# A two-layer graph kernel: diagonal blocks loaded once, and the norms and scaling of finished panels moved to other engines

## Chip, core and metric

The kernel runs on one core of one Trainium2 chip. The metric is the device time of one execution in microseconds: a median of 2270.47 us over 3 runs of the kernel before (2269.53 to 2271.97). TensorE is PE in the profile, VectorE DVE, ScalarE ACT, GpSimd POOL, and SyncE SP.

## What is computed

Everything is float32; N is 8192 rows, D is 128 columns, and adj is a full 8192 x 8192 matrix (256 MB).

```python
# layer 0
A = a * adj, with (1 - a) added to its diagonal
y = (A @ x) / A.sum(axis=1)
x1 = layernorm(x + relu(y @ W.T + b))
# layer 1, on x1
xt  = logmap0(x1)
par = adj   * sigmoid(xt @ wp[:D] [:, None] + xt @ wp[D:] [None, :] + b_par)
chi = adj.T * sigmoid(xt @ wc[:D] [:, None] + xt @ wc[D:] [None, :] + b_chi)
u   = chi @ xt + par @ xt
n   = max(norm(u), 1e-15)
e   = tanh(n) * u / n            # expmap0, then proj: norm at most 1 - 1e-5
out = layernorm(x1 + e * min(1, MAXNORM / norm(e)))
```

Layer 1 needs each block of adj twice: as it stands and turned. Of a block on the diagonal both are the same block of memory.

## The kernel before

adj is cut into 8 panels of 1024 output columns (`NPAN`, `BP`). A **unit** is one tile of 128 rows of layer 1 against one panel of 1024: 512 units. Two units share one load of 1 MB of the natural blocks (`a_cols`, kind "nat") and one of the turned ones (`g_blk`, kind "trn"). The loads go through a ring of 7 entries of 1 MB, to which three more in `xA` are added at the end of layer 0; `load_plan` writes the order out by hand, and SP issues each load once the last user of its entry is done (`wait_free`).

While layer 0 streams its 256 pairs, 154 units of the first three panels are interleaved. The other 358 units, from `N_EARLY` = 154, are the late stage. One unit of it is, on each engine:

- ACT: two sigmoids of 128x1024, one into `chi(n)` in SBUF (L646), one into a PSUM slot (L660). There are three slots; the sigmoid into a slot waits for the key of its last user.
- POOL: chi times the natural block (L494).
- DVE: the slot times the turned block (`first_product`, L914), then the sum of the two into `keys(n)` (`key`, L925).
- PE: two matmuls with `xtA`, accumulated in `outp` over a panel (L1125; four records each unit).

Panels 3 to 7 run 64 units each; between them the last 8 units of panels 0 to 2 are done. A group that ends releases its panel's **final**. Their base units b are 232, 266, 304, 338, 376, 410, 448 and 512 (`FINALS`), for the panels 3, 0, 4, 1, 5, 2, 6, 7. Of each final, the steps stand at fixed units after b (the constants `F_...`), written into each engine's order ahead of that unit's work:

- ACT copies `outp` to `uT` (L684; for the early panels it was done by L689), PE turns it by eight 128x128 transposes into a slot (`turn`, L1137), ACT copies the slot to `uN` in SBUF (L694) and takes eight squares with sums, one in each of eight units (L699).
- ACT takes the root of the eight sums (L707), together with the deviation of the final before (L712); each such visit needs a load of ACT's table and one back. DVE works out the factor in eight steps of 128x8 (`factor_step`, L939 to L953), with a tanh of ACT between steps 1 and 2 (L717).
- DVE turns the deviation of the final before into a factor and a shift (L973, L978), and ACT normalises that final's rows in eight pieces (L724), from b + 20 on.
- POOL scales `uN` by the factor (L510) and adds x1 (L516), at b + 29 and b + 31. DVE takes the statistics, one of eight in each of eight units (L960), and merges them (L967).

The chain of one final hangs on the next one's steps for its deviation and normalisation. The last final (b = 512) runs after the last unit, with nothing beside it.

Of the kernel before, what the change touches and what calls it, by code (L numbers as in the profile page):

```python
# [11 lines left out]
P = 128  # L12
# [48 lines left out]
def plan():  # L61

    unit_at, units, ends, waiting = {}, [], [], []
    groups = early_groups()
    for k, (p, tiles, a) in enumerate(groups):
        for jt in tiles:
            waiting.append((k, p, jt, (a + 1) * PPP + (T_OWN if p == a else T_UNITS)))
    for g in range(PAIRS):
        if waiting and waiting[0][3] <= g:
            k, p, jt, _ = waiting.pop(0)  # L70
            unit_at[g] = len(units)
            units.append((k, p, jt))
    n_early = len(units)
    units += [(k, p, jt) for k, p, jt, _ in waiting]
    order = []
    for k in range(EARLY, NPAN):
        order.append((k, range(UPP)))
        if k - EARLY < EARLY:
            order.append((k - EARLY, range((NPAN - 1) * TPP, UPP)))
    for p, tiles in order:  # L80
        groups.append((p, tiles, NPAN - 1))
        units += [(len(groups) - 1, p, jt) for jt in tiles]
    for n, (k, _, _) in enumerate(units):
        if n + 1 == len(units) or units[n + 1][0] != k:
            ends.append(n)
    return unit_at, units, n_early, groups, ends
# [5 lines left out]
LATE0 = N_EARLY  # L92

# [10 lines left out]
def finals():  # L104
# [30 lines left out]
def slot_plan():  # L135

    of_unit, of_final, holder, turn = {}, {}, {0: ("layer 0", 0), 1: ("passage", 0), 2: None}, 0
    starts = {b + F_SLOT: k for k, (_, b) in enumerate(FINALS)}
    uses = []
    for n in range(UNITS):  # L140
        if n in starts:
            uses.append(("final", starts[n], n))
        uses.append(("unit", n, n))
    uses.append(("final", len(FINALS) - 1, UNITS))
    last = 2
    for kind, i, n in uses:
        if n < SLOT_TWO:
            s = 2
        elif n < SLOT_THREE:
            s = 0 if last == 2 else 2  # L150
        else:
            s = (last + 1) % SB
        last = s
        (of_unit if kind == "unit" else of_final)[i] = (s, holder[s])
        holder[s] = (kind, i)
    return of_unit, of_final


SLOT_OF_UNIT, SLOT_OF_FINAL = slot_plan()
# [101 lines left out]
def adj_resnorm_kernel(nc, x_g, xT, g_blk, a_blk, WT, b_row, alpha, w_par, b_par, w_chi, b_chi, out):  # L261
    with ExitStack() as ctx:
# [38 lines left out]
        fs = sb("fs", [P, 11, UPP])  # L301
        mvf = sb("mvf", [P, UPP, 2])
        bstf = sb("bstf", [P, TPP, 6])
        s_n, s_nm, s_th, s_rn, s_s1, s_n2, s_s, s_sd, s_rs, s_mb, s_ss = [fs[:, k, :] for k in range(11)]
# [3 lines left out]
        uN = dsum[:, BP:2 * BP]  # L308
# [74 lines left out]
        p_ready = sem("p_ready")  # L383
        m1_ready = sem("m1_ready")
# [6 lines left out]
        uN_ready = sem("uN_ready")  # L391
# [5 lines left out]
        scaled = sem("scaled")  # L397
# [9 lines left out]
        N_CONST = 9  # L407

# [3 lines left out]
        def _(sp):  # L412
            def wait_free(e, before):
# [63 lines left out]
        def _(pool):  # L477
# [27 lines left out]
            def scale(k):  # L505
                at = slice(k * TPP, (k + 1) * TPP)
                u3 = uN.rearrange("p (t d) -> p t d", t=TPP)
                pool.wait_ge(f_step, f_steps(k, F_STEPS))
                pool.wait_ge(sq_ready, k + 1)
                pool.tensor_tensor(out=u3, in0=u3, in1=s_s[:, at].unsqueeze(2).to_broadcast([P, TPP, D]),  # L510
                                   op=ALU.mult).then_inc(scaled, 1)

            def add_residual(k):
                pool.wait_ge(scaled, k + 1)
                pool.wait_ge(x1f_in[k % 2], 16 * (k // 2 + 1))
                pool.tensor_tensor(out=x1f[k % 2][:, :], in0=uN, in1=x1f[k % 2][:, :], op=ALU.add).then_inc(v_ready, 1)  # L516

# [8 lines left out]
            for n in range(N_EARLY, UNITS):  # L526
                if n == LATE0 + 2 * T_FOLD:
                    fold(NPAN - 1)
                for k, (_, b) in enumerate(FINALS):
                    if n == b + F_SCALE:  # L530
                        scale(k)
                    if n == b + F_ADD:
                        add_residual(k)
# [3 lines left out]
            scale(NPAN - 1)  # L537
            add_residual(NPAN - 1)

        @block.scalar  # L540
        def _(act):
# [93 lines left out]
            def sigmoids(n):  # L635
# [12 lines left out]
                s, before = SLOT_OF_UNIT[n]  # L648
                if before is not None:
                    kind, i = before  # L650
                    if kind == "unit":
                        act.wait_ge(k_ready, i + 1)
                    elif kind == "final":
                        act.wait_ge(uN_ready, i + 1)
                    elif kind == "layer 0":
                        act.wait_ge(y_evac, NPAN)
                    else:
                        act.wait_ge(rows_ready, NPAN)
                        act.wait_ge(prcr_ready, NPAN)
                act.activation(slots[s], scores[:, row, 0, :], ACT.Sigmoid,  # L660
# [18 lines left out]
            def evacuate(k):  # L679
# [3 lines left out]
                act.wait_ge(sq_ready, k)  # L683
# [7 lines left out]
            def copy_turned(k):  # L691
                act.wait_ge(uT_ready, k + 1)
                act.wait_ge(v_ready, k)
                act.activation(uN, slots[SLOT_OF_FINAL[k][0]], ACT.Copy).then_inc(uN_ready, 1)  # L694

            def square(k, i):
                if i == 0:
                    act.wait_ge(uN_ready, k + 1)
                ins = act.activation(uT[:, i * D:(i + 1) * D], uN[:, i * D:(i + 1) * D], ACT.Square,  # L699
                                     accum_out=s_ss[:, k * TPP + i:k * TPP + i + 1])  # L700
                if i == TPP - 1:
                    ins.then_inc(sq_ready, 1)

            def norm(k):
                at = slice(k * TPP, (k + 1) * TPP)
                act.wait_ge(sq_ready, k + 1)
                act.activation(s_n[:, at], s_ss[:, at], ACT.Sqrt).then_inc(f_norm, 1)  # L707
# [20 lines left out]
            def final(k, step):  # L728
                if step == F_EVAC and FINALS[k][0] >= EARLY:
                    evacuate(k)  # L730
                if step == F_COPY:
                    copy_turned(k)
                if F_SQUARE <= step < F_SQUARE + TPP:
                    square(k, step - F_SQUARE)
# [53 lines left out]
            copy_turned(k)  # L788
            for i in range(TPP):
                square(k, i)  # L790
# [8 lines left out]
        def _(dve):  # L799
# [109 lines left out]
            def first_product(n):  # L909
                t, here, count = loaded("trn", n // 2)  # L910
                dve.wait_ge(here, count)
                dve.wait_ge(p_ready, n + 1)
                s = slots[SLOT_OF_UNIT[n][0]]
                dve.tensor_tensor(out=s, in0=s, in1=half(t, n), op=ALU.mult).then_inc(m1_ready, 1)  # L914

            def key(n):
                dve.wait_ge(m1_ready, n + 1)
                dve.wait_ge(m2_ready, n + 1)
                b, before = buffer_of(n, KB)
                if before is not None:  # L920
                    dve.wait_ge(kt_used, before + 1)
                elif b == KB:
                    dve.wait_ge(l0_used, PAIRS)
                    dve.wait_ge(res_ready, NPAN)
# [4 lines left out]
            def factor_step(k, i):  # L929
# [24 lines left out]
                ins.then_inc(f_step, 1)  # L954

# [25 lines left out]
            def final(k, i):  # L981
# [8 lines left out]
                if k > 0 and i == F_RSTD + 1:  # L990
                    final_shift(k - 1)
                if F_STATS <= i < F_STATS + TPP:
# [41 lines left out]
            for i in range(F_STEPS):  # L1034
                factor_step(k, i)
            for i in range(TPP):
# [6 lines left out]
        def _(pe):  # L1043
# [84 lines left out]


            def turn(k):  # L1130
                p, b = FINALS[k]
                pe.wait_ge(out_evac, GROUP_OF_FINAL[k] + 1)
                s, (kind, i) = SLOT_OF_FINAL[k]
                src = uT if p >= EARLY else acc[:, p * BP:(p + 1) * BP]
                pe.wait_ge(k_ready, i + 1)
# [55 lines left out]
```

## Time and profile before

| what | value |
|---|---|
| median of 3 runs | 2270.47 us (2269.53 to 2271.97) |
| profiled execution | 2267.84 us |
| its span, first to last instruction | 2266.0 us |
| busy: PE, DVE, ACT, POOL | 87%, 88%, 60%, 60% |
| bytes moved | 839.19 MB, 370 GB/s over the span |
| granted TensorE clock, mean | 0.972 |

An engine's row of the timeline gives an instruction's start and duration; two that follow each other without a wait overlap by some 0.1 us, so the cost of one is the distance between two starts. A releaser ("<-ACT ps L660") is whose semaphore ended the wait; "issue" means that the view found none.

### The profile page before, as it was taken

Reading aid. Unit: us, or ns where it says so; the run is one execution under the profiler, and the core shown is the slowest. Engines: PE = TensorE matmul, PEld = TensorE weight load, DVE = VectorE, ACT = ScalarE, POOL = GpSimd, SP = SyncE. Lnnn points to the kernel's source line nnn. Section 1 sums busy time; section 2 is a strip of 40 time slices with the busy share of each in tenths; the row PEclk is TensorE's granted clock in tenths of the full one; section 3 lists DMA queues with packets and bytes.
Section 4 is the critical chain, followed back from the end, with each engine's and each line's share of the span. In section 5 each row is a group of like instructions: output and inputs, shape, how many; then the busy total and the mean of one; then the engine's idle time right before and its main releaser. Section 6 shows DMA issues by size and latency. Waiting matters only on the chain. (4 is left out here: it accounts for less than half of the span.)

```text
span 2266.0 us, 17584 instructions
## 1 busy us (share of the span) xinstructions
PE 1964.4 (87%) x4652; PEld 829.8 (37%) x4652; DVE 1983.8 (88%) x1881; ACT 1349.4 (60%) x1640; POOL 1355.3 (60%) x559
## 2 busy tenths in 40 slices
PE   8999999999999989989999867887777778777774
PEld 3444444444444434434434323232222223222221
DVE  4676978988989988998999888999999999999995
ACT  0011324344364454453453687998889899898986
POOL 0000305436455455543444777999898998989995
PEclk9999999999999999999999988999999999999998
DMA  9998989899899988988888998999999999999993
GB/s 309 340 351 308 371 296 385 359 355 396 325 372 417 382 338 353 375 348 343 371 347 351 420 410 317 399 420 421 421 389 421 420 406 414 399 423 396 421 398 127
DMA packets 132083, 839.19 MB, mean 370 GB/s; under 512 B 15232, under 2 KB 27776, under 8 KB 33680
## 3 DMA queue, kind: packets, MB, share of 16 engines
q1 hardware_dynamic: 125184, 817.94, 90.5%
q10 hardware_dynamic: 6800, 20.13, 2.3%
q8 instruction: 38, 0.62, 0.1%
q14 instruction: 61, 0.50, 0.1%
HBM read 829.56 MB, written 8.45 MB: 370 GB/s over the span
## 5 line engine op out<-in xcount | busy, mean ns | idle before, releaser
L494 POOL TENSOR_TENSOR chi<-chi,ring 128x1024 f32<-128x1024 f32 x320 | 819.0, 2569 | 662.5 <-ACT chi L646 598.8
L1125 PE MATMUL ps<-keys,xtA 128*128 128x512 f32 x1720 | 847.1, 620 | 189.0 <-DVE keys L925 170.5
L1056 PE MATMUL ps<-ring,xA 128*128 128x512 f32 x2048 | 921.5, 600 | 37.1 <-DMA ring<-in_g_blk 32.9
L660 ACT ACTIVATE ps<-scores,prcr 128x1024 f32<-128x1024 f32 x512 | 567.8, 1109 | 435.9 <-DVE keys L925 417.4
L823 DVE TENSOR_TENSOR dsum<-dsum,ring 128x2048 f32<-128x2048 f32 x240 | 592.8, 2470 | 43.5 <-DMA ring<-in_g_blk 36.3
L914 DVE TENSOR_TENSOR ps<-ps,ring 128x1024 f32<-128x1024 f32 x440 | 537.7, 1222 | 66.6 <-ACT ps L660 62.7
L925 DVE TENSOR_TENSOR keys<-ps,chi 128x1024 f32<-128x1024 f32 x430 | 526.5, 1224 | 72.2 <-issue 39.4
L1056 PEld LDWEIGHTS ps<-ring,xA 128*128 128x128 f32 x2048 | 387.0, 192 | 531.3 <-issue 469.5
L1125 PEld LDWEIGHTS ps<-keys,xtA 128*128 128x128 f32 x1720 | 316.6, 195 | 688.2 <-issue 664.1
L646 ACT ACTIVATE chi<-scores,prcr 128x1024 f32<-128x1024 f32 x430 | 488.4, 1136 | 14.5 <-DMA scores<-plcl_d 6.7
L494 POOL TENSOR_TENSOR chi<-chi,xA 128x1024 f32<-128x1024 f32 x110 | 259.0, 2367 | 41.5 <-ACT chi L646 39.6
L1125 PE MATMUL ps<-xA,xtA 128*128 128x512 f32 x328 | 171.2, 647 | 49.1 <-DVE xA L925 33.6
L494 POOL TENSOR_TENSOR xA<-xA,ring 128x1024 f32<-128x1024 f32 x50 | 118.4, 2368 | 6.8 <-ACT xA L646 6.4
L1125 PEld LDWEIGHTS ps<-xA,xtA 128*128 128x128 f32 x328 | 60.4, 202 | 154.6 <-issue 135.0
L925 DVE TENSOR_TENSOR xA<-ps,xA 128x1024 f32<-128x1024 f32 x82 | 100.4, 1224 | 3.5 <-POOL xA L494 0.8
L487 POOL TENSOR_TENSOR dsum<-dsum 128x1024 f32<-128x1024 f32 x8 | 18.8, 2354 | 137.8 <-DVE dsum L823 137.8
L914 DVE TENSOR_TENSOR ps<-ps,xA 128x1024 f32<-128x1024 f32 x72 | 87.9, 1221 | 12.2 <-ACT ps L660 12.2
L646 ACT ACTIVATE xA<-scores,prcr 128x1024 f32<-128x1024 f32 x82 | 93.1, 1135 | 0.4 <-ACT yb L599 0.4
L558 ACT ACTIVATE small<-mv,epsc 128x8 f32<-128x8 f32 x8 | 2.4, 301 | 149.1 <-DVE mv L857 149.1
L494 POOL TENSOR_TENSOR xA<-xA 128x1024 f32<-128x1024 f32 x32 | 75.8, 2368 | 5.1 <-ACT xA L646 4.4
L819 DVE TENSOR_TENSOR dsum<-ring 128x1024 f32<-128x1024 f32 x16 | 34.4, 2186 | 31.4 <-PE ps L1065 17.2
L503 POOL TENSOR_TENSOR acc<-taken,acc 128x1024 f32<-128x1024 f32 x15 | 37.4, 2491 | 31.0 <-ACT taken L676 31.0
(99 smaller groups left out, 645.7 us busy)
## 6 DMA issues: line engine op xcount, KB each, us to landing
ring<-in_g_blk SPq DMA_DIRECT2D x476, 1024.0 KB, 9.8
ring<-in_a_cols SPq DMA_DIRECT2D x185, 1024.0 KB, 9.0
xA<-in_a_cols SPq DMA_DIRECT2D x71, 1024.0 KB, 9.5
xA<-in_g_blk SPq DMA_DIRECT2D x36, 1024.0 KB, 10.8
scores<-plcl_d ACTq DMA_DIRECT2D x22, 512.0 KB, 11.2
xA<-in_x_g SPq DMA_DIRECT2D x64, 64.0 KB, 13.2
yb<-in_xT ACTq DMA_DIRECT2D x8, 512.0 KB, 8.9
x_d<-res ACTq DMA_DIRECT2D x8, 512.0 KB, 9.0
```

Source lines behind the costliest of these rows:

```text
L487: pool.tensor_tensor(out=dsum[:, 0:BP], in0=dsum[:, 0:BP], in1=dsum[:, BP:2 * BP], op=ALU.add).then_inc(folded, 1)
L494: pool.tensor_tensor(out=chi(n), in0=chi(n), in1=half(t, n), op=ALU.mult).then_inc(m2_ready, 1)
L503: pool.tensor_tensor(out=at, in0=taken[:, :], in1=at, op=ALU.add).then_inc(acc_added, 1)
L558: act.activation(std, mv[:, :, 1], ACT.Sqrt, bias=epsc[:, 0:1]).then_inc(std_ready, 1)
L646: act.activation(chi(n), scores[:, row, 1, :], ACT.Sigmoid, bias=prcr[:, 2 * jt + 1:2 * jt + 2]).then_inc(c_ready, 1)
L660: act.activation(slots[s], scores[:, row, 0, :], ACT.Sigmoid, bias=prcr[:, 2 * jt:2 * jt + 1]).then_inc(p_ready, 1)
L819: dve.tensor_tensor(out=half(dsum, h), in0=half(t0, h), in1=half(t, h), op=ALU.add) \
L823: dve.tensor_tensor(out=dsum[:, :], in0=dsum[:, :], in1=t, op=ALU.add).then_inc(deg_added, 1)
L914: dve.tensor_tensor(out=s, in0=s, in1=half(t, n), op=ALU.mult).then_inc(m1_ready, 1)
L925: dve.tensor_tensor(out=keys(n), in0=slots[SLOT_OF_UNIT[n][0]], in1=chi(n), op=ALU.add).then_inc(k_ready, 1)
L1056: ins = pe.matmul(Y[:, h * BANK:(h + 1) * BANK], xA[:, tile * D:(tile + 1) * D], t[:, tt * BP + h * BANK:tt * BP + (h + 1) * BANK], start= ...
L1125: ins = pe.matmul(outp[:, h * BANK:(h + 1) * BANK], xtA[:, jt * D:(jt + 1) * D], keys(n)[:, h * BANK:(h + 1) * BANK], start=begins, stop=i ...
```

## The change

For the five late panels (3 to 7), the 8 units whose tile lies in the panel's own block ("own", 40 units in all, the list `OWN`) go last in their group. For those, the turned load is not made: 20 loads of 1 MB fewer. PE turns the natural block into the unit's PSUM slot instead (`turn_own`, eight transposes each unit, two units ahead), and ACT's sigmoid goes to one of two SBUF buffers (`own_par`: `taken` and the piece of `xA` that was the fourth buffer of `keys`). `keys` has three buffers throughout.

Of a finished panel, ACT squares the unturned `uT` (or `acc`) in one instruction into `sqT`, PE sums the squares over the partitions by eight matmuls with a column of ones into a slot (`norms`), and ACT takes the root from there. PE turns the panel into another slot later, and DVE multiplies by the factor and adds x1 in eight instructions that read PSUM (`add_residual`). ACT's copy and eight squares, and POOL's two instructions, are gone. The steps stand at new places.

```diff
+        if len(tiles) == UPP:
+            own = range(p * TPP, (p + 1) * TPP)
+            tiles = [jt for jt in tiles if jt not in own] + list(own)
-F_EVAC, F_TURN, F_SLOT, F_COPY, F_SQUARE, F_ROOT, F_FLOOR, F_INV, F_RSTD, F_TANH, F_CHAIN, F_NORM, F_SCALE, F_ADD, \
-    F_STATS, F_AGGR = 3, 2, 4, 5, 6, 15, 17, 18, 18, 19, 21, 20, 29, 31, 33, 42
+F_EVAC, F_SQUARE, F_NORMS, F_NORMS_SLOT, F_ROOT, F_FLOOR, F_INV, F_RSTD, F_TANH, F_CHAIN, F_NORM, F_TURN, F_SLOT, \
+    F_ADD, F_STATS, F_AGGR = 3, 4, 4, 6, 7, 8, 9, 9, 12, 11, 13, 14, 16, 17, 18, 26
-F_STORE = 42
-L_ROOT, L_RSTD, L_NORM = 47, 49, 52
+F_STORE = 36
+L_ROOT, L_RSTD, L_NORM = 34, 36, 38
-        kinds += [("nat", c), ("trn", c)]
+        kinds += [("nat", c)] if 2 * c in OWN_AT else [("nat", c), ("trn", c)]
-            b, _ = buffer_of(n, KB)
-            return keys_few[:, b, :] if b < KB else xA[:, EXTRA * CH + BP:EXTRA * CH + 2 * BP]
+            return keys_few[:, n % KB, :]
+        own_par = [taken[:, :], xA[:, EXTRA * CH + BP:EXTRA * CH + 2 * BP]]
...
+                    if 2 * j in OWN_AT:
+                        sp.wait_ge(own_turned, (OWN_AT[2 * j] // TPP + 1) * TPP)
...
-            scale(NPAN - 1)
-            add_residual(NPAN - 1)
...
+                if n in OWN_AT:
+                    i = OWN_AT[n]
+                    if i >= 2:
+                        act.wait_ge(m1_ready, OWN[i - 2] + 1)
...
+            def square(k):
+                p, _ = FINALS[k]
+                act.wait_ge(out_evac, GROUP_OF_FINAL[k] + 1)
+                act.wait_ge(norms_ready, k)
+                act.activation(sqT, uT if p >= EARLY else acc[:, p * BP:(p + 1) * BP], ACT.Square).then_inc(sq_ready, 1)
...
+                if n in OWN_AT:
+                    dve.wait_ge(own_turned, OWN_AT[n] + 1)
+                    other = own_par[OWN_AT[n] % 2]
...
+            def add_residual(k):
+                dve.wait_ge(f_step, f_steps(k, F_STEPS))
+                dve.wait_ge(uT_ready, k + 1)
+                dve.wait_ge(x1f_in[k % 2], 16 * (k // 2 + 1))
+                for i in range(TPP):
+                    t, j = x1f[k % 2][:, i * D:(i + 1) * D], k * TPP + i
+                    ins = dve.scalar_tensor_tensor(out=t, in0=slots[SLOT_OF_FINAL[k][0]][:, i * D:(i + 1) * D],
+                                                   scalar=s_s[:, j:j + 1], in1=t, op0=ALU.mult, op1=ALU.add)
+                ins.then_inc(v_ready, 1)
...
+            def turn_own(n):
+                s, before = SLOT_OF_UNIT[n]
+                slot_free(pe, before)
+                for k in range(TPP):
+                    (t, here, count), h = natural_of_own(n, k)
+                    pe.wait_ge(here, count)
+                    ins = pe.transpose(columns(slots[s], k), columns(half(t, h), UNIT[n][2] % TPP), ident[:, :])
+                ins.then_inc(own_turned, 1)
+
+            def norms(k):
+                pe.wait_ge(sq_ready, k + 1)
+                s, before = SLOT_OF_NORMS[k]
+                slot_free(pe, before)
+                for j in range(TPP):
+                    ins = pe.matmul(slots[s][:, j:j + 1], columns(sqT, j), ones[:, 0:1], start=True, stop=True)
+                ins.then_inc(norms_ready, 1)
...
+                    if n == b + F_NORMS:
+                        norms(k)
...
+                if n + 2 in OWN_AT:
+                    turn_own(n + 2)
```

## Rows read from the trace of the kernel before

**Rows 1.** The page: busy time of each engine, then GB/s in 40 slices.

```profile
PE 1964.4 (87%) x4652; PEld 829.8 (37%) x4652; DVE 1983.8 (88%) x1881; ACT 1349.4 (60%) x1640; POOL 1355.3 (60%) x559
...
GB/s 309 340 351 308 371 296 385 359 355 396 325 372 417 382 338 353 375 348 343 371 347 351 420 410 317 399 420 421 421 389 421 420 406 414 399 423 396 421 398 127
```

**Rows 2.** L914 in two windows: us, busy (count), clock, DMA share, GB/s.

```profile
1422.90:1494.90 72.00, 36.67 (x30) 0.99 1.00 413
1494.90:2237.10 742.20, 340.53 (x279) 0.97 0.99 405
```

**Rows 3.** DVE's waits, 1494.9 to 2237.1: us in total, times, longest.

```profile
DVE keys L925 <- issue: 13.1, 6, 2.2
DVE ps L914 <- ACT ps L660: 11.9, 17, 2.1
DVE keys L925 <- DVE ps L914: 4.1, 7, 0.6
DVE keys L925 <- POOL chi L494: 3.5, 14, 0.3
```

**Rows 4.** DVE's groups there: count, busy us, mean ns, idle before.

```profile
L943 DVE TENSOR_TENSOR fs<-fs 128x8 f32<-128x8 f32 x7 | 9.5, 1358 | 0.0
...
L939 DVE TENSOR_SCALAR fs<-fs 128x8 f32<-128x8 f32 x7 | 7.3, 1041 | 0.0
...
L945 DVE TENSOR_TENSOR fs<-fs 128x8 f32<-128x8 f32 x7 | 3.2, 462 | 0.0
...
L960 DVE BATCH_NORM_STATS2 bstf<-yb 128x6 f32<-128x128 f32 x32 | 9.1, 284 | 0.0
...
L967 DVE BATCH_NORM_AGGREGATE mvf<-bstf 128x2 f32<-128x6 f32 x56 | 4.4, 151 | 0.0
```

**Rows 5.** Timeline, first final: start, us, engine, operation, idle before.

```profile
1550.02 4.65 POOL L494 TENSOR_TENSOR chi<-chi,ring 128x1024 f32<-128x1024 f32 x2
...
1554.63 2.35 POOL L494 TENSOR_TENSOR xA<-xA,ring 128x1024 f32<-128x1024 f32 x1
...
1554.71 2.30 DVE L945 TENSOR_TENSOR fs<-fs 128x8 f32<-128x8 f32 x1
```

**Rows 6.** Timeline of the third final, ACT's square root and normalisation.

```profile
1723.95 1.28 ACT L707 ACT_TABLE_LOAD   x1
...
1729.21 1.23 DVE L914 TENSOR_TENSOR ps<-ps,ring 128x1024 f32<-128x1024 f32 x1 [2.09 <-ACT ps L660]
...
1740.33 0.49 ACT L724 ACTIVATE res<-res,fs 128x128 f32<-128x128 f32 x1 [2.77 <-DVE fs L978]
```

**Rows 7.** Timeline of DVE, the eight products that read PSUM in layer 0.

```profile
1304.19 2.15 DVE L845 SCALAR_TENSOR_TENSOR res<-ps,small,bb 128x128 f32<-128x128 f32 x8
```

**Rows 8.** Timeline of PE around a turn, and the degree sums' matmuls.

```profile
1501.74 1.88 PE L1125 MATMUL ps<-keys,xtA 128*128 128x512 f32 x4
1503.46 1.11 PE L1137 MATMUL ps<-ident,dsum 128*128 128x128 f32 x8
1504.41 1.88 PE L1125 MATMUL ps<-keys,xtA 128*128 128x512 f32 x4
...
1274.94 1.70 PE L1065 MATMUL ps<-ones,dsum 128*128 128x1 f32 x14
```

**Rows 9.** Timeline of the last final, after the last unit.

```profile
2241.74 1.02 ACT L684 ACTIVATE dsum<-ps 128x1024 f32<-128x1024 f32 x1 [7.57 <-PE ps L1125]
...
2248.89 0.21 ACT L707 ACTIVATE fs<-fs 128x8 f32<-128x8 f32 x1
...
2252.01 1.90 POOL L510 TENSOR_TENSOR dsum<-dsum,fs 128x1024 f32<-128x1024 f32 x1 [15.37 <-DVE fs L953]
...
2256.36 1.65 DVE L960 BATCH_NORM_STATS2 bstf<-res 128x6 f32<-128x128 f32 x8 [4.42 <-POOL res L516]
```

**Rows 10.** What the SP queue waited for from 1494.9 to 2237.1.

```profile
SPq L470 <- POOL chi L494: 493.2, 133, 6.4
```

**Rows 11.** Issues of that window: KB each, us from issue to landing.

```profile
ring<-in_a_cols SPq DMA_DIRECT2D x81, 1024.0 KB, 9.7
```

More of the change, by code:

```diff
@@ L92 @@
 LATE0 = N_EARLY
+OWN = [n for n in range(N_EARLY, UNITS) if UNIT[n][1] >= EARLY and UNIT[n][2] // TPP == UNIT[n][1]]
+OWN_AT = {n: i for i, n in enumerate(OWN)}
 def is_first(n):
@@ L135, in slot_plan @@
 def slot_plan():
-    of_unit, of_final, holder, turn = {}, {}, {0: ("layer 0", 0), 1: ("passage", 0), 2: None}, 0
-    starts = {b + F_SLOT: k for k, (_, b) in enumerate(FINALS)}
+    plans = {"unit": {}, "norms": {}, "final": {}}
+    holder = {0: ("layer 0", 0), 1: ("passage", 0), 2: None}
+    starts = {b + F_NORMS_SLOT: ("norms", k) for k, (_, b) in enumerate(FINALS)}
+    starts |= {b + F_SLOT: ("final", k) for k, (_, b) in enumerate(FINALS)}
     uses = []
@@ L141, in slot_plan @@
         if n in starts:
-            uses.append(("final", starts[n], n))
+            uses.append(starts[n] + (n,))
         uses.append(("unit", n, n))
-    uses.append(("final", len(FINALS) - 1, UNITS))
+    uses += [("norms", len(FINALS) - 1, UNITS), ("final", len(FINALS) - 1, UNITS)]
     last = 2
@@ L153, in slot_plan @@
         last = s
-        (of_unit if kind == "unit" else of_final)[i] = (s, holder[s])
+        plans[kind][i] = (s, holder[s])
         holder[s] = (kind, i)
-    return of_unit, of_final
-SLOT_OF_UNIT, SLOT_OF_FINAL = slot_plan()
+    return plans["unit"], plans["norms"], plans["final"]
+SLOT_OF_UNIT, SLOT_OF_NORMS, SLOT_OF_FINAL = slot_plan()
 def load_plan():
@@ L300, in adj_resnorm_kernel @@
          dg, sf, rc, inv, mb) = [small[:, k, :] for k in range(21)]
-        fs = sb("fs", [P, 11, UPP])
+        fs = sb("fs", [P, 10, UPP])
         mvf = sb("mvf", [P, UPP, 2])
         bstf = sb("bstf", [P, TPP, 6])
-        s_n, s_nm, s_th, s_rn, s_s1, s_n2, s_s, s_sd, s_rs, s_mb, s_ss = [fs[:, k, :] for k in range(11)]
+        s_n, s_nm, s_th, s_rn, s_s1, s_n2, s_s, s_sd, s_rs, s_mb = [fs[:, k, :] for k in range(10)]
         uT = dsum[:, 0:BP]
-        uN = dsum[:, BP:2 * BP]
+        sqT = dsum[:, BP:2 * BP]
         x1f = [yb, res]
@@ L407, in adj_resnorm_kernel, with slot_free @@
         N_CONST = 9
+        def slot_free(eng, before):
+            kind, i = before
+            if kind == "unit":
+                eng.wait_ge(k_ready, i + 1)
+            elif kind == "norms":
+                eng.wait_ge(f_norm, i + 1)
+            elif kind == "final":
+                eng.wait_ge(v_ready, i + 1)
+            elif kind == "layer 0":
+                eng.wait_ge(y_evac, NPAN)
+            else:
+                eng.wait_ge(rows_ready, NPAN)
+                eng.wait_ge(prcr_ready, NPAN)
         block = ctx.enter_context(nc.Block())
@@ L647, in sigmoids @@
                                bias=prcr[:, 2 * jt + 1:2 * jt + 2]).then_inc(c_ready, 1)
[L648 to L656, printed above, removed]
-                    else:
-                        act.wait_ge(rows_ready, NPAN)
-                        act.wait_ge(prcr_ready, NPAN)
-                act.activation(slots[s], scores[:, row, 0, :], ACT.Sigmoid,
+                if n in OWN_AT:
+                    i = OWN_AT[n]
+                    if i >= 2:
+                        act.wait_ge(m1_ready, OWN[i - 2] + 1)
+                    elif i == 1:
+                        act.wait_ge(l0_used, PAIRS)
+                        act.wait_ge(res_ready, NPAN)
+                    else:
+                        act.wait_ge(acc_added, ADDED_ALL)
+                    dst = own_par[i % 2]
+                else:
+                    s, before = SLOT_OF_UNIT[n]
+                    if before is not None:
+                        slot_free(act, before)
+                    dst = slots[s]
+                act.activation(dst, scores[:, row, 0, :], ACT.Sigmoid,
                                bias=prcr[:, 2 * jt:2 * jt + 1]).then_inc(p_ready, 1)
@@ L730, in final @@
                     evacuate(k)
[L731 to L734, printed above, removed]
+                if step == F_SQUARE:
+                    square(k)
                 if step == F_ROOT:
@@ L787, in _ @@
             evacuate(k)
-            copy_turned(k)
-            for i in range(TPP):
-                square(k, i)
+            square(k)
             norm(k)
@@ L909, in first_product @@
             def first_product(n):
-                t, here, count = loaded("trn", n // 2)
-                dve.wait_ge(here, count)
+                s = slots[SLOT_OF_UNIT[n][0]]
+                if n in OWN_AT:
+                    dve.wait_ge(own_turned, OWN_AT[n] + 1)
+                    other = own_par[OWN_AT[n] % 2]
+                else:
+                    t, here, count = loaded("trn", n // 2)
+                    dve.wait_ge(here, count)
+                    other = half(t, n)
                 dve.wait_ge(p_ready, n + 1)
-                s = slots[SLOT_OF_UNIT[n][0]]
-                dve.tensor_tensor(out=s, in0=s, in1=half(t, n), op=ALU.mult).then_inc(m1_ready, 1)
+                dve.tensor_tensor(out=s, in0=s, in1=other, op=ALU.mult).then_inc(m1_ready, 1)
             def key(n):
@@ L918, in key @@
                 dve.wait_ge(m2_ready, n + 1)
[L919 to L924, printed above, removed]
+                if n >= KB:
+                    dve.wait_ge(kt_used, n - KB + 1)
                 dve.tensor_tensor(out=keys(n), in0=slots[SLOT_OF_UNIT[n][0]], in1=chi(n),
@@ L991, in final @@
                     final_shift(k - 1)
+                if i == F_ADD:
+                    add_residual(k)
                 if F_STATS <= i < F_STATS + TPP:
@@ L1127, in products @@
                 ins.then_inc(kt_used, 1)
+            def turn_own(n):
+                s, before = SLOT_OF_UNIT[n]
+                slot_free(pe, before)
[11 more added lines that the diff above has]
+                ins.then_inc(norms_ready, 1)
             def turn(k):
```

44 lines of the change are left out of this document (10 added, 34 removed).

## The prediction, made before the changed kernel ran

> **What bounds the kernel now.** I first read the page: DVE is the busiest engine over the span, with PE one point behind, and the transfers run at 420 GB/s in most slices of the second half [rows 1]. The change touches only the late stage, so I then took that stage alone, by the starts of L914, one in each unit. In 72.0 us without a final there are 30 units, 2.40 us each [rows 2]. DVE's two instructions take 1.22 us each and overlap by some 0.1 us, so DVE has no pause there: it is the bound. From unit 232 to the last, 279 units take 742.2 us [rows 2]. At 2.40 us they would take 669.6, so the first seven finals cost DVE 72.6 us. That is the sum that the change alters, and after it comes the tail of the eighth final. Of the 72.6 us:
> - Waits, 33.4 us. The six "issue" waits of 2.2 us and the seven of 0.6 us (17.2 us) come two to four units after POOL's scaling and addition: POOL's product is late because of them. The 11.9 us for ACT's sigmoid and the 4.3 us for POOL's product behind it (3.5 in [rows 3], 0.8 in one more row) come after ACT's final work: 16.2 us [rows 3].
> - Statistics: 56 at 0.28 us, less the overlap of 0.09, and 56 merges at 0.07 apart: 14.7 us [rows 4].
> - What is left, 24.5 us, is DVE's 128x8 instructions, although one that doesn't wait takes 0.16 us. They wait for POOL: L945 began at 1554.71, when POOL had begun a product at 1554.63, and lasted until that product ended, 2.30 us [rows 5]. L939 takes 1.04 us in all seven, L943 1.36 us on average, L945 0.46 on average, which is one of 2.3 us in the first final and 0.16 in the six others, and L951 does the same [rows 4]. So the first final pays 7.4 us here and each of the others 2.9.
>
> No transfer ends a wait of DVE [rows 3], and SP mostly waits for POOL to free an entry [rows 10]: loads are early.
>
> **The transfers.** 20 loads of 1 MB go, with nothing late that waits for them: I count zero. If they did set the pace, see the third rival.
>
> **Own units on PE.** A turn fills 0.95 us of PE (1503.46 to 1504.41) and a unit's matmuls 1.72 (1501.74 to 1503.46) [rows 8]: 2.67 us for an own unit, against 2.40 of DVE. PE falls behind by 0.27 us a unit, 1.9 us after seven turns. A turn is issued two units ahead and, without a lag, is done 3.0 us after the start of DVE's unit n - 2, that is 1.8 us before it is needed. So the lag just fits: no stall. The last two units have no turn, so PE enters the final 0.8 us late. The bound on the other side: were a turn's last natural block to land only when it is needed, the turn comes 1.1 us late and DVE follows PE's 2.67 us for 8 units: 3.3 us for each of five groups, 16 us. The last of the four natural loads of a group gets the entry of a turned load four pairs ahead, free 7 units or 16.8 us before the first own unit's product, and lands 9.7 us later [rows 11]: 7 us early, and 4 before PE wants it. So I take zero. Three `keys` buffers instead of four: PE's restart after ACT's copy of the early panel becomes a limit only if DVE is less than three units behind, and DVE is late there itself: zero.
>
> **DVE's new work.** Eight instructions on PSUM with a pointer scalar and one SBUF input are L845's form: 2.15 us for eight [rows 7], also with POOL busy beside them. Seven finals: +15.1 us. These do not wait for POOL, as their second input is a scalar, and the trace's eight didn't. The Trainium skill ("SBUF — State Buffer", Who interferes with whom) says why: a DVE instruction with at most one SBUF tensor input doesn't contend with GpSimd, while with two the later one blocks for the whole of the other's instruction. Had they contended, one wait of up to 2.3 us would come with each final, +16 us.
>
> **POOL's work goes.** The 17.2 us of waits behind it go. -17.2 us.
>
> **ACT's work shrinks.** Copy and eight squares become one square of about 1.05 us. But the visit to the square root stays: 1.28 + 0.21 + 0.28 + 1.28 us, 3.1 together, from 1723.95 [rows 6]. It moves from b + 15 to b + 7, and the norms' slot, taken at unit 6, makes unit 6's sigmoid wait for key 4. That sigmoid starts at b + 12.1 us, the root's visit lasts from 13.2 to 16.2, unit 7's second sigmoid starts at 17.3, and DVE starts 1.2 us behind it, at 18.5 instead of 16.8: 1.7 us. The eight sums on PE (16 records at 0.12 us, 2.0 us [rows 8]) end at about 13.4 to 14.6, under the table load. Seven times 1.7 is 11.9, with 0.14 us behind each at the key: 12.9 us, where there were 16.2. -3.3 us.
>
> **The 128x8 instructions.** Their number is the same, but what makes them cheap now? In the later finals ACT stands still for 2.77 us at b + 20, until DVE has the shift [rows 6]. POOL then starves and goes in step with DVE, each product ending just as DVE's next short instruction comes. After the change the shift is at b + 10 and its reader at b + 13: no standstill. That is the first final's case, which has no earlier final to normalise: ACT runs ahead, POOL goes back to back at 2.31 us, and DVE, 2.40 us from the end of one blocked instruction to the next, finds POOL just started again [rows 5]. So I follow POOL from unit 7 on: step 0 waits 1.1 us as now; the shift at b + 10 meets a product begun 0.2 us before, 2.1 us; step 2 at b + 11 the next one, 2.2 us, except where the early panel's copy, 1.0 us of ACT, has delayed POOL (0.1); step 3 0.1 to 0.5; step 4 0.1 or 2.2; the rest 0.6. That gives 4.0 to 6.3 us for two finals, 6.4 to 8.6 for four, and 8.1 for the first: some 46 us, where there are 24.5. +21.5 us. The ends: 2.9 us each as now, 20 us in all (-4.5); 8.6 each, 60 us (+36).
>
> **The tail.** The root ends at 2249.1 [rows 9]. Afterwards: `outp` copied from 2241.74 + 0.8 (PE's lag) = 2242.5, 1.05; square, 1.05; sums, 2.0; root at 2246.7, 2.2 us earlier. From the factor (2252.01) to the statistics (2256.36) it takes 4.35 us through POOL [rows 9], and 2.2 through DVE: 2.1 us earlier. -4.3 us.
>
> **Sum.** 15.1 - 17.2 - 3.3 + 21.5 - 4.3 = +11.8. Against the profiled execution (2267.84 us, span 2266.0) that is 2279.6. The runs' median is 2.6 us above it, so 2282.3 as the metric goes.
>
> **Rivals.**
> - Cheap short instructions. They keep falling into POOL's gaps, 20 us in all. Then the sum is 15.1 - 17.2 - 3.3 - 4.5 - 4.3 = -14.2 us, 2256.3. For: six of seven finals show it. Against: the standstill that brought it about goes. It decides as soon as POOL waits for ACT's sigmoid between b + 10 and b + 13.
> - In between: POOL is caught in half of the cases, 35 us, so +0.8 us, 2271.3.
> - The transfers set the pace. The rate is 421 GB/s in 100 us stretches and the DMA share 0.99 [rows 1, 2]; at 2.49 us for each MB, 20 loads are 50 us, 2220. Against: no DMA row among the waits, and 2.40 us, less than 2.49, in the stretch without a final. The Trainium skill ("SBUF — State Buffer", Summary: rules for kernel authors) gives some 358 GB/s for transfers from HBM; by that figure the loads would be the bound by far, 59 us for the 20. The trace shows 405 over the stage, and the trace decides.
> - Late turns. The case of the natural blocks above, 16 us on top: 2298. For: the first turn of a group needs all four natural loads, and these entries are kept until the eighth turn. Against: the landings.
>
> **How the numbers follow.** Forecast 0.50, cheap 0.20, in between 0.17, late turns 0.10, transfers 0.03. The forecast's own range is 2271 to 2291 (35 to 55 us for the short instructions). The range reaches from the cheap case to the late turns: 2257 to 2298. Faster by over 0.2%, 4.5 us (about what a measurement of this kernel can tell from no change): cheap and transfers, 0.24 with a little of the middle. Within: 0.19, the middle and the edge of the forecast. Slower: 0.57.
>
> **What would show it.** L914's 279 intervals: 742 us now, some 758 if I am right. L939 at about 1.1 us, L978 no longer 0.16 but near 2, L943 near 2 in five finals; L516's "issue" waits gone; one wait for ACT of some 1.7 us at b + 7; the eight L845-like instructions at 2.15; no wait of DVE for PE's turns. If L978 and L943 stay short, the cheap case holds. If DVE waits for PE in the own groups, the late turns do. I would be wrong altogether if 2.40 us a unit itself changes.

## The result, and the profile after

| what | before | after |
|---|---|---|
| median | 2270.0 us (4 runs, 2266.4 to 2271.97) | 2294.36 us (4 runs, 2290.93 to 2297.57) |
| ratio of after to before | | 1.0107 [1.0087, 1.0126] |
| profiled execution, its span | 2267.84, 2266.0 us | 2295.63, 2293.8 us |
| granted TensorE clock, mean | 0.972 | 0.965 |

The change costs 24.4 us. The forecast was 2282.3, so the direction was right and the loss is twice the predicted one. The page shows DVE 50 us busier than before and POOL 34 us less busy (against [rows 1]):

```profile
PE 2020.7 (88%) x5100; PEld 896.8 (39%) x5100; DVE 2034.3 (89%) x1945; ACT 1335.3 (58%) x1512; POOL 1321.7 (58%) x543
```

**Where the time is.** The starts of L924 (L914 before) in the same two windows as [rows 2]: us, busy (count), granted clock, DMA share, GB/s.

```profile
1424.10:1496.30 72.20, 36.69 (x30) 0.99 0.90 363
1496.30:2268.20 771.90, 340.56 (x279) 0.95 0.91 367
```

A unit without a final still takes 2.41 us, with a tenth of the transfers' share gone: that stretch did not hang on the loads. The 279 units take 771.9 us instead of 742.2, so seven finals cost 771.9 - 669.6 = 102.3 us instead of 72.6. That is +29.7. Unit 232 starts 1.4 us later, and what follows the last unit takes 2293.8 - 2268.2 = 25.6 us instead of 28.9, -3.3; together 27.8, which is the difference of the two spans.

DVE's waits in that window (total, times, longest), to set beside [rows 3]:

```profile
DVE ps L924 <- ACT ps L677: 11.3, 8, 1.6
DVE keys L931 <- POOL chi L528: 1.8, 7, 0.3
DVE ps L924 <- PE ps L1154: 0.5, 3, 0.2
DVE keys L931 <- DVE ps L924: 0.5, 1, 0.5
DVE keys L931 <- PE ps L1144: 0.3, 1, 0.3
```

They sum to 14.4 us, where there were 33.4. The waits behind POOL's scaling are gone; the one for PE's own turns is 0.5 us. DVE's groups, beside [rows 4] (count, busy us, mean ns, idle before):

```profile
L949 DVE TENSOR_TENSOR fs<-fs 128x8 f32<-128x8 f32 x7 | 15.9, 2272 | 0.0
L953 DVE TENSOR_SCALAR fs<-fs 128x8 f32<-128x8 f32 x7 | 14.1, 2014 | 0.0
L994 DVE SCALAR_TENSOR_TENSOR fs<-mvf,fs 128x8 f32<-128x8 f32 x7 | 12.8, 1831 | 0.0
...
L968 DVE SCALAR_TENSOR_TENSOR yb<-ps,fs,yb 128x128 f32<-128x128 f32 x32 | 8.6, 341 | 0.0
L945 DVE TENSOR_SCALAR fs<-fs 128x8 f32<-128x8 f32 x7 | 7.8, 1113 | 0.0
...
L951 DVE TENSOR_TENSOR fs<-fs 128x8 f32<-128x8 f32 x7 | 5.8, 828 | 0.0
```

Five instructions of 128x8 (the clamp L945, steps 2 to 4 at L949 to L953, the shift L994) are busy for 56 us, where each would be 0.16 us if nothing held it. The timeline of the third final shows what holds them (start, us):

```profile
1724.58 2.08 DVE L994 SCALAR_TENSOR_TENSOR fs<-mvf,fs 128x8 f32<-128x8 f32 x1
...
1726.58 1.22 DVE L924 TENSOR_TENSOR ps<-ps,ring 128x1024 f32<-128x1024 f32 x1
1726.58 2.38 POOL L528 TENSOR_TENSOR xA<-xA,ring 128x1024 f32<-128x1024 f32 x1
...
1728.90 2.36 POOL L528 TENSOR_TENSOR chi<-chi,ring 128x1024 f32<-128x1024 f32 x1
1728.97 2.32 DVE L949 TENSOR_TENSOR fs<-fs 128x8 f32<-128x8 f32 x1
...
1736.44 2.35 POOL L528 TENSOR_TENSOR chi<-chi,xA 128x1024 f32<-128x1024 f32 x1 [2.29 <-ACT chi L660]
1736.49 2.33 DVE L953 TENSOR_SCALAR fs<-fs 128x8 f32<-128x8 f32 x1
```

The shift ends with POOL's product, DVE does one unit (2.39 us to L949's start), POOL one product (2.32), and L949 arrives 0.07 us after the next product began. It waits that one out. It is the picture of [rows 5], now three times in each of six finals: L994, L949 and L953. The first final has no shift; there L949, L951 and the last step are held (2.07, 2.32 and 2.37 us). L953 is caught in another way than L949: POOL had not been working back to back but had stood still for 2.29 us, waiting for ACT, and began its product 0.05 us before L953 came.

The ends agree throughout. In the 279 units, 35 of DVE's 128x8 instructions took more than 0.25 us (reciprocals left aside), and each of them ended 0.02 to 0.03 us behind the end of a POOL product. The other 14 met no product that went on for longer than they did. The kernel before gives the same picture with 17 and 32.

The account of the 102.3 us, with the predicted terms beside it: statistics 14.7 (as before); the eight PSUM products 7 x 2.07 = 14.5 (predicted 15.1); waits 14.4, that is -19.0 (predicted -17.2 - 3.3 = -20.5); what is left, the short instructions, 58.7 us, that is +34.2 (predicted +21.5, upper end +36).

### The profile page after: what moved, and what is told of

It is laid out like the page before. It is cut to its first block, busy times and chain, and to the rows that moved or that the text cites. A ratio compares the mean times of both kernels' runs of the same rounds, so it can differ in the third digit from the quotient of the medians.

```text
span 2293.8 us, 18436 instructions
## 1 busy us (share of the span) xinstructions
PE 2020.7 (88%) x5100; PEld 896.8 (39%) x5100; DVE 2034.3 (89%) x1945; ACT 1335.3 (58%) x1512; POOL 1321.7 (58%) x543
## 4 chain that ended last, share of the span: by engine, by line
PE 36%; DVE 21%; issue 15%; POOL 15%; ACT 9%; DMA 3%; DVEq 0%; ACTq 0%; SPq 0%; POOLq 0%
PE ps L1075 24%; POOL chi L528 11%; PE ps L1144 9%; DVE ps L924 8%; DVE dsum L828 5%; ACT chi L660 3%; DMA ring<-in_g_blk 3%; POOL xA L528 3%; DVE keys L931 2%; ACT ps L677 2%; PE ps L1154 2%; ACT L660 1%; POOL acc L537 1%; DVE dsum L824 1%; DVE fs L953 1%
## 5 line engine op out<-in xcount | busy, mean ns | idle before, releaser
L1144 PE MATMUL ps<-keys,xtA 128*128 128x512 f32 x2048 | 1023.9, 631 | 216.1 <-DVE keys L931 188.0
L1075 PE MATMUL ps<-ring,xA 128*128 128x512 f32 x2048 | 921.5, 600 | 38.3 <-DMA ring<-in_g_blk 34.2
L677 ACT ACTIVATE ps<-scores,prcr 128x1024 f32<-128x1024 f32 x472 | 524.1, 1110 | 475.7 <-DVE keys L931 456.2
L1144 PEld LDWEIGHTS ps<-keys,xtA 128*128 128x128 f32 x2048 | 383.7, 199 | 789.9 <-issue 751.6
L924 DVE TENSOR_TENSOR ps<-ps,ring 128x1024 f32<-128x1024 f32 x410 | 501.1, 1222 | 68.3 <-ACT ps L677 65.5
L660 ACT ACTIVATE chi<-scores,prcr 128x1024 f32<-128x1024 f32 x430 | 488.2, 1135 | 14.4 <-DMA scores<-plcl_d 6.9
L528 POOL TENSOR_TENSOR chi<-chi,xA 128x1024 f32<-128x1024 f32 x107 | 251.8, 2367 | 50.7 <-ACT chi L660 49.5
L924 DVE TENSOR_TENSOR ps<-ps,xA 128x1024 f32<-128x1024 f32 x82 | 100.2, 1222 | 11.8 <-ACT ps L677 11.0
L931 DVE TENSOR_TENSOR keys<-ps,xA 128x1024 f32<-128x1024 f32 x82 | 100.4, 1225 | 3.0 <-POOL xA L528 0.2
L603 ACT ACTIVATE xtA<-res,small 128x128 f32<-128x128 f32 x64 | 19.6, 388 | 48.5 <-DVE small L890 48.5
```

The lines of the kernel that those rows point to most:

```text
L528: pool.tensor_tensor(out=chi(n), in0=chi(n), in1=half(t, n), op=ALU.mult).then_inc(m2_ready, 1)
L660: act.activation(chi(n), scores[:, row, 1, :], ACT.Sigmoid, bias=prcr[:, 2 * jt + 1:2 * jt + 2]).then_inc(c_ready, 1)
L677: act.activation(dst, scores[:, row, 0, :], ACT.Sigmoid, bias=prcr[:, 2 * jt:2 * jt + 1]).then_inc(p_ready, 1)
L924: dve.tensor_tensor(out=s, in0=s, in1=other, op=ALU.mult).then_inc(m1_ready, 1)
L931: dve.tensor_tensor(out=keys(n), in0=slots[SLOT_OF_UNIT[n][0]], in1=chi(n), op=ALU.add).then_inc(k_ready, 1)
L1075: ins = pe.matmul(Y[:, h * BANK:(h + 1) * BANK], xA[:, tile * D:(tile + 1) * D], t[:, tt * BP + h * BANK:tt * BP + (h + 1) * BANK], start= ...
```

## The experiments

What they had to tell apart: whether the loss lies in the finals' short instructions alone, whether those were cheap before because ACT stood still behind the shift (the prediction's reason), and what makes one of them cheap or dear. Each ratio is to runs of the kernel before on the same chip.

**The standstill taken out of the kernel before.** Normalising three units later, ACT no longer waits for the shift.

```diff
-    F_STATS, F_AGGR = 3, 2, 4, 5, 6, 15, 17, 18, 18, 19, 21, 20, 29, 31, 33, 42
+    F_STATS, F_AGGR = 3, 2, 4, 5, 6, 15, 17, 18, 18, 19, 21, 23, 29, 31, 33, 42
```

> The kernel before with one constant changed: the normalisation of the final before starts at b + 23 instead of b + 20, so ACT no longer stands still for 2.77 us at b + 20 until DVE has the shift. Theory A (the short 128x8 instructions are cheap in the kernel before only because that standstill puts POOL in step with DVE): L943, L945 or L951 rise to near 2 us in the six later finals, some 3 to 6 us for each, 15 to 30 us slower, 2285 to 2300. Rival B (their price has nothing to do with the standstill): unchanged or up to 4 us faster, as ACT no longer waits, 2266 to 2270.

Measured: 2258.05 us, ratio 0.9947 [0.9933, 0.9962]. It got faster, against my expectation. Groups and waits of DVE over the same 279 units, and the timeline of the third final:

```profile
L978 DVE SCALAR_TENSOR_TENSOR fs<-mvf,fs 128x8 f32<-128x8 f32 x7 | 12.8, 1834 | 0.0
...
L943 DVE TENSOR_TENSOR fs<-fs 128x8 f32<-128x8 f32 x7 | 2.9, 421 | 0.0
```

```profile
DVE ps L914 <- ACT ps L660: 10.3, 11, 2.1
DVE keys L925 <- DVE ps L914: 3.6, 7, 0.6
DVE keys L925 <- POOL chi L494: 2.8, 11, 0.3
```

```profile
1738.93 2.09 DVE L978 SCALAR_TENSOR_TENSOR fs<-mvf,fs 128x8 f32<-128x8 f32 x1
...
1740.94 4.68 POOL L494 TENSOR_TENSOR chi<-chi,ring 128x1024 f32<-128x1024 f32 x2
...
1745.73 0.16 DVE L943 TENSOR_TENSOR fs<-fs 128x8 f32<-128x8 f32 x1
...
1746.17 2.36 POOL L494 TENSOR_TENSOR chi<-chi,ring 128x1024 f32<-128x1024 f32 x1 [0.54 <-ACT chi L646]
```

One half of the theory holds: without the standstill the shift goes from 0.16 to 2.09 us. The other half does not: L943 became cheaper, 0.42 us on average instead of 1.36. Here two units lie between the shift and step 2, where the kernel after has one. In the second of them POOL, which makes its product in 2.32 us where DVE needs 2.40 and more, has run out of ACT's sigmoids and waits (0.54 us); the short instruction falls into that gap, 0.16 us, in six of the seven finals. In the first, which has no shift, it still takes 2.01 us. And the six "issue" waits of [rows 3], 13.1 us, are not in the list any more. They had come behind POOL's scaling and addition, which are still there; with the standstill gone POOL makes up for them. By what link, no run separates. The seven finals cost 732.1 - 669.6 = 62.5 us, 10.1 less than before.

**One half of the change at a time.** The own units and their turns put into the kernel before; and the kernel after without them (all loads, new finals).

```diff
-OWN = [n for n in range(N_EARLY, UNITS) if UNIT[n][1] >= EARLY and UNIT[n][2] // TPP == UNIT[n][1]]
+OWN = []
```

> The kernel before with the first half of the change alone: own units last in their group, turned by PE, 20 loads fewer, three keys buffers; the finals as before. Theory A (all of the loss is in the finals): within 3 us of before, 2267 to 2273. Rival B (PE's turns, or the burst of loads after a group, hold DVE up): 5 to 16 us slower, with waits of DVE for PE or DMA in the own units. Rival C (fewer loads help): up to 50 us faster.

> The changed kernel with the second half alone: every turned block loaded, no own units; norms on PE, scaling on DVE, steps at their new places. Theory A: the whole loss stays, 2291 to 2296, with 14.4 us over 2.40 us a unit for each final. Rival B (half of the loss is the own blocks): 2278 to 2285.

Measured: own units alone 2271.85 us, 1.0009 [0.9997, 1.0021]; finals alone 2292.1 us, 1.0101 [1.0082, 1.0119]. The 279 units in each, own units alone first:

```profile
1499.00:2242.20 743.20, 340.62 (x279) 0.98 0.93 381
```

```profile
1496.50:2267.30 770.80, 340.45 (x279) 0.95 0.96 390
```

The whole loss is in the finals, to within what these runs can tell. Turning the diagonal blocks costs nothing that can be measured, and the loads saved bring nothing: the DMA share falls from 0.99 to 0.93 and the 279 units take 743.2 us instead of 742.2.

**Normalising at once in the kernel after.** ACT goes to the normalisation at b + 11 and must wait for the shift, as it did before.

```diff
-    F_ADD, F_STATS, F_AGGR = 3, 4, 4, 6, 7, 8, 9, 9, 12, 11, 13, 14, 16, 17, 18, 26
+    F_ADD, F_STATS, F_AGGR = 3, 4, 4, 6, 7, 8, 9, 9, 12, 11, 11, 14, 16, 17, 18, 26
```

> The changed kernel with one constant changed: normalisation from b + 11 instead of b + 13, so that ACT waits for DVE's shift (b + 10) as it did in the kernel before. Theory A (a standstill of ACT brings POOL in step): ACT waits 1 to 3 us there and L943, L945, L951 fall to near 0.2 us in most finals, 3 to 6 us less for each of six, 2260 to 2276. Rival B: no step changes, or the standstill adds to it, 2294 to 2305. In between: L978 itself stays blocked, as it comes before the standstill.

Measured: 2267.79 us, ratio 0.9988 [0.9975, 1.0]: 26.6 us better than the kernel after, by adding a wait of ACT. The timeline of the third final:

```profile
1726.61 0.16 DVE L994 SCALAR_TENSOR_TENSOR fs<-mvf,fs 128x8 f32<-128x8 f32 x1
...
1726.80 0.49 ACT L733 ACTIVATE res<-res,fs 128x128 f32<-128x128 f32 x1 [2.67 <-DVE fs L994]
...
1729.38 2.35 POOL L528 TENSOR_TENSOR chi<-chi,ring 128x1024 f32<-128x1024 f32 x1 [3.05 <-ACT chi L660]
...
1736.64 0.16 DVE L953 TENSOR_SCALAR fs<-fs 128x8 f32<-128x8 f32 x1
```

ACT stands still for 2.67 us, POOL starves for 3.05, and both the shift and L953 drop to 0.16 us (L949 keeps 1.28 in the six later finals). The finals cost 744.1 - 669.6 = 74.5 us in all, about what they cost before (72.6); 4.3 us of it are new, DVE waiting for ACT's tanh.

**Two more units between shift and step 2.** Three units lie between them here, where the kernel after has one (the expectation says two). If the distance that the first experiment showed is the cause, it must work here without any standstill. The steps behind move along.

```diff
-    F_ADD, F_STATS, F_AGGR = 3, 4, 4, 6, 7, 8, 9, 9, 12, 11, 13, 14, 16, 17, 18, 26
+    F_ADD, F_STATS, F_AGGR = 3, 4, 4, 6, 7, 8, 9, 9, 12, 13, 13, 16, 18, 19, 20, 28
```

> The changed kernel with steps 2 to 7 from b + 13 on instead of b + 11, so that two units lie between the shift (b + 10) and step 2; turn, addition and statistics two units later. Refined theory (an instruction that follows a blocked one by one unit is blocked again, since DVE takes 2.40 us and POOL 2.31; with two units between, POOL has caught up with ACT and waits for it, as in the kernel before with its normalisation at b + 23): L949, L951 and L953 near 0.2 to 1.3 us, 3 to 5 us less for each of seven finals, 2258 to 2275. Rival (the place within the panel doesn't matter, POOL is always inside a product): 2290 to 2298.

Measured: 2268.17 us, ratio 0.9984 [0.9968, 1.0]. Groups of DVE, and the third final:

```profile
L994 DVE SCALAR_TENSOR_TENSOR fs<-mvf,fs 128x8 f32<-128x8 f32 x7 | 12.8, 1833 | 0.0
...
L949 DVE TENSOR_TENSOR fs<-fs 128x8 f32<-128x8 f32 x7 | 4.5, 645 | 0.0
...
L953 DVE TENSOR_SCALAR fs<-fs 128x8 f32<-128x8 f32 x7 | 1.2, 167 | 0.0
```

```profile
1728.42 4.83 POOL L528 TENSOR_TENSOR chi<-chi,xA 128x1024 f32<-128x1024 f32 x2 [0.52 <-ACT chi L660]
...
1730.38 0.43 DVE L949 TENSOR_TENSOR fs<-fs 128x8 f32<-128x8 f32 x1
```

The shift is as dear as in the kernel after (1833 ns), but POOL has waited 0.52 us for ACT by the time step 2 comes, so that L949 meets a product 1.96 us after its start and waits out only the rest. It falls from 2272 to 645 ns on average, L953 from 2014 to 167. So the place of a short instruction sets its price, and a standstill of ACT is one way to a cheap place, not the only one. Distance alone is no rule: in the first final L949 still takes 1.95 us, five units after the last held one, as POOL had been working back to back.

**The short instructions on POOL.** An instruction on POOL can't be held by POOL. Steps 0, 2, 3, 4, 6, 7 and the shift (now two instructions) move there, the reciprocals stay on DVE; the same for the kernel before. The steps also come up to three units later, which the lines below do not show.

```diff
-                if F_CHAIN <= i < F_CHAIN + F_STEPS - 2:
-                    factor_step(k, i - F_CHAIN + 2)
+                if i == F_RECIP:
+                    factor_step(dve, k, 5)
...
+                    if n - b in P_STEP:
+                        factor_step(pool, k, P_STEP[n - b])
+                    if k > 0 and n == b + P_SHIFT:
+                        final_shift(pool, k - 1)
```

> The changed kernel with six of the eight factor steps and the shift (two instructions there) on POOL instead of DVE, in POOL's own order, so that they can't be blocked by POOL's product; the two reciprocals stay on DVE, and the places of the steps are some units later, since the engines hand over. Theory A (60 us of the changed kernel's 102 over 2.40 us a unit are DVE standing behind POOL's products at these steps): some 50 to 57 us less, 2237 to 2246, faster than both kernels; each final at 6 to 7 us over 2.40 a unit. Rival B (POOL has no room: it is busy 2.31 us of each 2.40, and seven more instructions for each final make its products late): DVE waits at the key instead, 2260 to 2290.

> The kernel before with the same edit. Theory A: of its 24.5 us of short instructions 22 go, 2245 to 2252. Rival B: POOL's scaling and addition are still there, its products come later by the added instructions, and DVE waits for them: 2262 to 2275.

Measured: in the kernel after 2251.66 us, ratio 0.992 [0.9896, 0.9944], 42.7 us less than the kernel after; in the kernel before 2259.47 us, 0.9959 [0.9945, 0.9973]. The seven finals cost 729.4 - 669.6 = 59.8 us in the first. The gain is less than the theory's 50 to 57 us, and its range (2237 to 2246) was missed. One of POOL's groups there, DVE's wait for ACT that is left, and the timeline of one such wait in the third final:

```profile
L466 POOL TENSOR_SCALAR fs<-fs 128x8 f32<-128x8 f32 x7 | 1.8, 256 | 0.6
```

```profile
DVE ps L969 <- ACT ps L722: 19.8, 14, 1.6
```

```profile
1732.23 1.12 ACT L722 ACTIVATE ps<-scores,prcr 128x1024 f32<-128x1024 f32 x1 [4.63 <-DVE yb L987]
...
1733.45 1.23 DVE L969 TENSOR_TENSOR ps<-ps,ring 128x1024 f32<-128x1024 f32 x1 [1.25 <-ACT ps L722]
```

What cost up to 2.3 us on DVE costs 0.20 to 0.26 us on POOL. With DVE's waits at 26.7 us in all, the account leaves 59.8 - 14.7 - 14.5 - 26.7 = 3.9 us for what short instructions DVE still has, where it was 58.7. DVE's waits rose from 14.4 us, which took 12.3 of that gain back. Later places alone (the experiment above, at other units) gave 2268, so by these two runs the engine's own share of the 42.7 us is some 16. In the kernel before the same edit gives only 11 us, between what the two theories expected: there the waits behind POOL's scaling grew.

```profile
DVE keys L970 <- issue: 28.0, 14, 2.5
```

They were 13.1 in [rows 3]. Two come with each final, one behind the scaling and one behind the addition. That the short steps on POOL cause them, and not the moved places, is not shown. With the steps off DVE the new finals are the faster ones: 2251.7 against 2259.5.

**A slot held shorter.** Of the 19.8 us above, 7 x 1.25 = 8.8 come from the sigmoid that waits 4.63 us for DVE's eight products to free the slot of the turned panel. The turn goes two units later, and its slot is taken one unit later.

```diff
-    F_ADD, F_STATS, F_AGGR = 3, 4, 4, 6, 7, 9, 10, 10, 12, 11, 14, 15, 18, 20, 21, 29
+    F_ADD, F_STATS, F_AGGR = 3, 4, 4, 6, 7, 9, 10, 10, 12, 11, 14, 17, 19, 20, 21, 29
```

> The kernel with POOL's short steps, and the turned panel's slot taken one unit later (b + 19 instead of b + 18) and the turn two units later. There, ACT's sigmoid of unit b + 20 waited for the slot that DVE's eight products were still reading, 4.63 us, and DVE then 1.25 to 1.4 us for ACT, once a final. Theory: unit b + 21 takes that slot instead, and some 1.3 us go for each of seven finals, 9 us less, 2240 to 2245; each final at about 7.2 us over 2.40 us a unit. Rival (the wait moves on to unit b + 21 and stays): 2249 to 2254.

Measured: 2241.86 us (4 runs, 2239.39 to 2247.7), ratio 0.9866 [0.9849, 0.9882]. It beats both kernels, the one before by 28 us (2269.98 in these rounds). The waits for ACT, 8.8 us fewer:

```profile
DVE ps L969 <- ACT ps L722: 11.0, 7, 1.6
```

The seven that are left are behind the root's table loads. A final now costs 50.1 / 7 = 7.2 us (719.7 us for the 279 units), where it was 10.4 before and 14.6 after.

**The same with all loads.** Do the saved 20 MB matter once DVE is this fast?

> The same without own units: every turned block is loaded, 20 loads more. Theory (loads stay hidden even at this pace): within 4 us of the run beside it. Rival (the transfers become the bound: 72 units and two finals take some 187 us now, and their 76 MB at 421 GB/s take 189): 3 to 15 us slower than the run beside it, with waits of DVE or POOL for loads, so the saved loads pay only once the finals are cheap.

Measured: 2244.33 us, ratio 0.9879 [0.9864, 0.9894]; 2.5 us more than with the turns, in intervals that overlap. The page's rate in 40 slices, and the loads among DVE's waits:

```profile
GB/s 313 342 359 304 380 291 381 362 349 390 361 336 414 393 331 364 362 348 344 370 350 336 422 420 313 388 421 420 421 421 420 422 421 420 421 421 421 421 422 175
```

```profile
DVE ps L966 <- DMA ring<-in_g_blk: 1.5, 2, 1.0
DVE ps L966 <- DMA xA<-in_g_blk: 0.5, 1, 0.5
```

From slice 27 on the transfers run at 420 GB/s nearly to the end, and for the first time in these late stages DVE waits for loads, 2.0 us. The 279 units take 722.1 us against 719.7 with the turns. So the two bounds come close here, and the diagonal half of the change may begin to pay; 2.4 us in one trace each, and medians that can't be told apart, do not show it.

## Why the prediction was right or wrong

- **Bound, account, transfers.** Right: 2.40 us a unit stayed, no load was waited for, and 20 loads fewer brought nothing (own units alone, 1.0009).
- **Own turns at zero.** Right: a turned unit is 2.67 us on PE here too, and DVE waited 0.5 us for turns in all. The timeline of PE in the last own group before unit 232:

```profile
1474.11 1.11 PE L1154 MATMUL ps<-ident,ring 128*128 128x128 f32 x8
1475.06 1.88 PE L1144 MATMUL ps<-keys,xtA 128*128 128x512 f32 x4
1476.78 1.11 PE L1154 MATMUL ps<-ident,ring 128*128 128x128 f32 x8
```

- **DVE's products.** 15.1 predicted, 14.5 measured; they never waited for POOL, as the Trainium skill's rule ("SBUF — State Buffer", Who interferes with whom) has it for one SBUF input. The prediction left out the rule's condition, that the instruction is outside the 2-port modes. One SBUF input alone did not protect the `tensor_scalar` steps: L945 and L953 were held (1.11 and 2.3 us).
- **POOL's and ACT's waits.** -20.5 predicted, -19.0 measured: POOL's 17.2 went, and the root's visit costs 1.6 us in each final (7 x 1.6 = 11.3 with one small one), as worked out.
- **The short instructions, the term that was mis-sized.** Predicted 46 us, measured 58.7; with it the forecast's own range, 2271 to 2291, was left by 3 us, and the whole range held. (The middles of the prediction's own three groups add up to 48.4, not 46.) The places were right (clamp 1.1 us, shift 2.1, step 2 2.2). Two sizes were not. Step 2 was put at 0.1 us in two finals, on the early panel's copy delaying POOL; it was blocked in all seven (mean 2272 ns). And step 4 was left at "0.1 or 2.2" and counted as cheap in some; it was 2.3 in six (mean 2014 ns). L949 comes one unit after the held shift. As DVE's unit is 2.40 us and POOL's product 2.32, back to back, being caught once makes it likely to be caught again one unit later. L953 in the third final was caught after POOL had waited 2.29 us for ACT, whose sigmoid into the slot had itself waited 2.06 us for DVE's key: there ACT's chain set POOL's start, 0.05 us ahead of L953. The prediction followed POOL only as working back to back. I had followed POOL by single starts and let margins of 0.1 us decide; two of them fell the other way.
- **The reason for the old cheapness.** Half right. The standstill kept the shift cheap, and put back into the kernel after it is worth 26.6 us. But it wasn't needed for step 2 (the first experiment), and the kernel before is 13 us better off without it (2258.05 against 2271.41). What the runs leave is plainer: a short instruction costs what is left of POOL's product when it comes. Whether POOL worked back to back or had waited for ACT does not decide it by itself. In the first experiment L943 fell into such a wait and took 0.16 us; L953 in the kernel after came just behind the end of one and took 2.3.
- **The tail.** -4.3 predicted, -3.3 measured. The sums took 3.19 us instead of 2.0, as the granted clock fell some 0.5 us into them, behind a pause of 2.20 us (see the last section):

```profile
2268.13 5.32 PE L1144 MATMUL ps<-keys,xtA 128*128 128x512 f32 x12
...
2275.64 3.19 PE L1163 MATMUL ps<-ones,dsum 128*128 128x1 f32 x16 [2.20 <-ACT dsum L711]
```

- **Rivals.** None came true. "Cheap short instructions" is what the experiments at b + 11 and b + 13 make of the kernel; both end at 2268, not at 2256, since the clamp and one or two others stay dear, and at b + 11 the wait for the tanh comes on top.

What stays open: which of POOL's products a short instruction meets is decided by less than 0.1 us in some places (L949 arrives 0.07 us after a start), and no run here shifts a single arrival by that much. The start of unit 232 lies anywhere from 1489.8 to 1503.3 us in these kernels; the stage before it was not studied. That POOL holds DVE is read from ends that coincide, in all 35 cases of the kernel after, and from the experiment that took the short instructions off DVE; no run took POOL's product away.

## What to carry to other kernels

Price a tiny instruction by what the neighbouring engine is doing when it comes, not by its size: here 0.16 us, or up to 2.3 when it met the start of POOL's product. Where two engines run in step with almost the same period, one that is held sets the place of the next. Moving the steps by two units won 26 us here, but the place has to be read from the trace again, as L953 was held although its neighbour had waited for ACT. Putting them on the engine that does the holding took away 54.8 of the 58.7 us, though new waits of DVE took 12.3 of that back. The work that the change moved from POOL onto DVE, the bound, paid only after DVE had been rid of what held it.

## What the runs showed of the hardware

- The reciprocals of 128x8 on DVE took 0.19 us in every final, whatever POOL did, while a `tensor_scalar` of the same shape, with one input too, took 2.01 on average (L953). All seven of L947 came 0.05 to 0.08 us after the start of a POOL product, just where L949 and L953 were held for 2.3 us. The Trainium skill ("SBUF — State Buffer", Who interferes with whom) counts `tensor_scalar` among the operations that can contend with GpSimd, and L953 agrees. Two groups of the kernel after:

```profile
L955 DVE RECIPROCAL fs<-fs 128x8 f32<-128x8 f32 x7 | 1.4, 193 | 0.0
L947 DVE RECIPROCAL fs<-fs 128x8 f32<-128x8 f32 x7 | 1.3, 193 | 0.0
```

- After 2.20 us without work PE began at the higher of its two levels and dropped to the lower one 0.5 us later: us, PE busy (count), granted clock of the kernel after, before the pause, at the start of the sums, and further on.

```profile
2266.00:2273.00 7.00, 7.00 (x24) 1.00 0.00 0
2275.60:2276.10 0.50, 0.46 (x4) 1.00 0.00 0
2277.00:2279.00 2.00, 2.00 (x11) 0.50 0.00 0
```

The drop is from 2.4 to 1.2 GHz, between 2276.1 and 2276.5, with PE busy without a break in the 7 us ahead of the pause and again behind it.
